# A three-part sequence kernel on one core: the matrix inversion on diagonal blocks of 64, the attention mask written in the scores' tiles, and a new order of the work

## The chip, the cores and the metric

The kernel runs on one core of a Trainium2 chip. Its engines work side by side, each through its own list of instructions in order: TensorE (PE: matrix products and transposes, with PEld for its weight loads), VectorE (DVE), ScalarE (ACT), GpSimd (POOL), and SyncE (SP), which here only issues transfers. They wait for one another by semaphores. Products land in PSUM, which has eight banks; everything else is in SBUF. The metric is the device time of one execution in microseconds (us). Lower is better.

## The reference, cut to what matters

Input is `x` of 2048 tokens by 128 features, all float32. Two parts follow each other:

```python
x = x + layernorm(scan(layernorm(x), W0, Wkv, bkv, eta))
x = x + layernorm(net(layernorm(x), ...))
# scan over the 2048 tokens, one after the other:
y = xt @ W.T;  err = y - vt;  W = W - eta * 2/128 * (err.T @ xt)
# net: 6 layers, 16 heads of 64, window 32
for i in range(6):
    x = attn(shift(x)) + x        # q, k: l2norm, scale, rotary; scores in windows of 32
    x = ffn(shift(x)) + x         # layernorm, W1, a * gelu(gate), W2
# in the attention:
sim = where(mask, -max, q @ k.T * 8);  out = softmax(sim) @ v;  out = out @ Wo
```

The scan updates a 128x128 matrix by one token at a time. The kernel does it in 16 chunks of 128 tokens: inside a chunk the token by token dependence is a unit lower triangular system, and its 128x128 matrix has to be inverted once for each chunk.

## The kernel before, in words

A chunk or tile is 128 tokens; there are 16 tiles, in four groups of four.

**Start.** Tokens are normalised and transposed, and `gram` forms each chunk's matrix of inner products. The triangular matrices of the 16 chunks are inverted together by doubling: six rounds (`ROUNDS`), each with `below(r, g)` (a product with the masked part `c_b`, made by GpSimd), a copy of the product by ScalarE (`c_q`), `update(r, g)` (two products, for the inverse and its transpose, `c_mm`), and a subtraction on VectorE. `targets` makes the values of the scan on the way. In the last round only one of the two is updated. `apply_x` and `apply_v` use the inverses, and the short chain `chain_w`, VectorE `chain_u`, `chain_d`, VectorE `chain_W` walks through the 16 chunks, four before the main loop and four each in its first three steps (`chunk_at`).

**Main loop.** 96 tile visits (6 layers of 16 tiles) and 14 more steps to run out. Each engine's body is one list written by hand; `t = s - lag` says which tile a piece serves, so one pass through the list works on several tiles at once. For each tile TensorE does: `project` (k halves, then q halves, four products 128x128 by 512 columns into `psq`), `turn` twice (the normalised k and q are transposed, T0 to T3), `values` for the four windows (U0 to U3), `mask` and `scores` into `pss`, `turn_p` (P0, P1), and `mix` (Y). For each group of four tiles it does once: transposes F and X, six `hidden` products (gates G0 to G2, and A0 to A2), and `narrow` (Z). `merge` makes a layer's 16 combined value and output matrices from `mvT` and `wo` as four banks H0 to H3, once a layer.

The mask is a product that starts the accumulation in each half of `pss`: in `mask`, two bf16 products of 512 columns, with 32 rows and 128 output partitions each (a tile's shape of 32x128 on the array), or with the identity for the first tile of a layer. The 64 products of `scores` then accumulate onto it, in the shape 64x32: two halves of the rows by four quarters of the columns, eight positions. Products with the same shape but different positions can run at once on the array; `values` and `mix` use 128x32, the turns and merges 64x128, `project`, `hidden` and `narrow` the whole 128x128.

**Buffers.** Outside `psq` and `pss` (two banks each) four banks form a ring. `take` gives them out in TensorE's order, so the bank of a product is that of four products before, and TensorE waits until ScalarE or VectorE has emptied it (`freed`). `psq` is held by the k halves until VectorE has read it twice (lines 782 and 785) and ScalarE has squared it (1167), then by the q halves (841, 857, 1062).

**The roots.** The norms' inverse roots for 32 heads of q and k: ScalarE makes a first guess from the bits of the sum (line 1094, `SEED`), and GpSimd refines it by ten small operations, lines 1269 to 1287, each waiting for the one before. Then GpSimd scales k and q (1290, 1294).

**ScalarE's tables.** Exp (1134) and Gelu (1158) need different function tables, and the compiler puts a table load before a use whose table is not in place. The three Gelus of a group stand together, behind the Exp of their step.

## Time and profile before

| | |
|---|---|
| median of 3 runs | 1675.6 us (1674.8 to 1677.26) |
| the profiled execution: its time, its span | 1674.12 us, 1672.3 us |
| mean granted TensorE clock | 0.985 of full speed |
| PE, busy and share of the span | 1591.6 us, 95% |
| DVE | 1253.5 us, 75% |
| ACT | 1080.7 us, 65% |
| POOL | 1386.3 us, 83% |
| PEld (weight loads, beside PE) | 938.3 us, 56% |

A row of a timeline gives the start in the span, the duration of the piece, the engine, the line, what is written from what, the shape on the array (rows*columns) and the count of instructions in the piece. A float32 product or weight load is two instructions here. Consecutive pieces overlap a little, since a product's end is modelled; what a piece costs is the difference between its start and the next one's. The bracket at the end is the idle time before the piece and who ended it.

### The profile page before, as it was taken

Reading aid. Unit: us, or ns where it says so; the run is one execution under the profiler, and the core shown is the slowest. Engines: PE = TensorE matmul, PEld = TensorE weight load, DVE = VectorE, ACT = ScalarE, POOL = GpSimd, SP = SyncE. Lnnn points to the kernel's source line nnn. Section 1 sums busy time; section 2 is a strip of 40 time slices with the busy share of each in tenths; the row PEclk is TensorE's granted clock in tenths of the full one; section 3 lists DMA queues with packets and bytes.
Section 4 is the critical chain, followed back from the end, with each engine's and each line's share of the span. In section 5 each row is a group of like instructions: output and inputs, shape, how many; then the busy total and the mean of one; then the engine's idle time right before and its main releaser. Section 6 shows DMA issues by size and latency. Waiting matters only on the chain.

```text
span 1672.3 us, 67208 instructions
## 1 busy us (share of the span) xinstructions
PE 1591.6 (95%) x29072; PEld 938.3 (56%) x29072; DVE 1253.5 (75%) x1683; ACT 1080.7 (65%) x1843; POOL 1386.3 (83%) x1726
## 2 busy tenths in 40 slices
PE   5986899999999999999999999999999999999994
PEld 4963455655555555565555555555555555555552
DVE  5447777777787787787787787777777787778863
ACT  3234766767766776766766767676766766766661
POOL 6318898988988988988998988988998998988971
PEclk9987999999999999999999999999999999999998
DMA  5000000010000010000010000010000000000000
GB/s 191 2 26 1 28 9 8 3 59 9 3 22 9 3 59 9 3 21 9 3 59 9 3 22 9 3 59 9 3 22 9 2 10 9 4 21 9 7 11 26
DMA packets 24534, 32.70 MB, mean 20 GB/s; under 512 B 2372, under 2 KB 21424, under 8 KB 23344
## 3 DMA queue, kind: packets, MB, share of 16 engines
q1 hardware_dynamic: 24240, 28.41, 5.2%
q8 instruction: 230, 3.77, 0.9%
q14 instruction: 64, 0.52, 0.1%
HBM read 21.06 MB, written 1.05 MB: 13 GB/s over the span
## 4 chain that ended last, share of the span: by engine, by line
PE 82%; POOL 8%; issue 5%; DVE 3%; ACT 1%; DMA 0%; SPq 0%; POOLq 0%; DVEq 0%; ACTq 0%
PE psq L245 19%; PE ring L265 18%; PE ring L253 9%; PE ring L300 9%; PE ring L310 8%; PE pss L284 7%; PE ring L317 3%; PE pss L276 1%; PE ring L326 1%; PE ring L355 1%; POOL qa L1290 1%; POOL qa L1245 1%; POOL qa L1236 1%; POOL qa L1294 1%; POOL pr L1240 1%
## 5 line engine op out<-in xcount | busy, mean ns | idle before, releaser
L245 PE MATMUL psq<-wqk,x0S 128*128 128x512 f32 x768 | 383.0, 622 | 5.5 <-ACT x0S L990 3.7
L265 PE MATMUL ring<-mh,x0S 128*32 128x512 f32 x3072 | 367.2, 595 | 0.4 <-ACT uT L1158 0.4
L1245 POOL TENSOR_TENSOR qa<-qa,qb 128x1024 f32<-128x1024 f32 x96 | 228.3, 2378 | 65.6 <-DVE qb L857 65.5
L1236 POOL TENSOR_TENSOR qa<-qa,qb 128x1024 f32<-128x1024 f32 x96 | 226.9, 2364 | 6.8 <-DVE qb L785 6.8
L245 PEld LDWEIGHTS psq<-wqk,x0S 128*128 128x128 f32 x768 | 136.1, 192 | 133.0 <-issue 117.2
L253 PEld LDWEIGHTS ring<-ident,qa 64*128 64x128 f32 x3072 | 110.5, 139 | 158.8 <-issue 104.7
L866 DVE TENSOR_REDUCE ss<-sq 128x16 f32<-128x1024 f32 x96 | 117.1, 1220 | 104.0 <-ACT sq L1062 104.0
L300 PE MATMUL ring<-u,pT 128*32 128x128 f32 x6144 | 187.6, 274 | 3.8 <-ACT pT L1129 3.5
L1290 POOL TENSOR_TENSOR qa<-qa,rn 128x1024 f32<-128x1024 f32 x96 | 182.7, 1903 | 7.5
L1240 POOL TENSOR_TENSOR pr<-pr,rden 128x1024 f32<-128x1024 f32 x96 | 184.0, 1916 | 2.0 <-DVE rden L814 2.0
L1294 POOL TENSOR_TENSOR qa<-qa,rn 128x1024 f32<-128x1024 f32 x96 | 183.2, 1908 | 0.0
L300 PEld LDWEIGHTS ring<-u,pT 128*32 128x32 f32 x6144 | 162.0, 110 | 27.2 <-issue 27.2
L284 PEld LDWEIGHTS pss<-kT,qT 64*32 64x32 f32 x12288 | 127.9, 105 | 83.3 <-issue 82.2
L782 DVE TENSOR_TENSOR qa<-psq,tab 128x1024 f32<-128x1024 f32 x96 | 117.2, 1221 | 75.4 <-PE psq L245 75.2
L1051 ACT COPY qT<-ring 128x512 f32<-128x512 f32 x96 | 56.3, 586 | 157.3 <-PE ring L253 157.3
L265 PEld LDWEIGHTS ring<-mh,x0S 128*32 128x32 f32 x3072 | 87.9, 109 | 123.1 <-issue 107.4
L841 DVE TENSOR_TENSOR qa<-psq,tab 128x1024 f32<-128x1024 f32 x96 | 117.2, 1221 | 51.1 <-PE psq L245 51.1
L310 PE MATMUL ring<-xh,w 128*128 128x512 f32 (+1 forms) x288 | 146.7, 620 | 1.4 <-ACT xh L1147 0.9
L284 PE MATMUL pss<-kT,qT 64*32 64x64 f32 x12288 | 144.5, 226 | 3.3 <-issue 3.3
L253 PE MATMUL ring<-ident,qa 64*128 64x64 f32 x3072 | 136.7, 229 | 6.4 <-POOL qa L1290 5.3
L1062 ACT ACTIVATE sq<-psq 128x1024 f32<-128x1024 f32 x96 | 98.3, 1023 | 67.7 <-DVE qb L857 67.7
L1167 ACT ACTIVATE sq<-psq 128x1024 f32<-128x1024 f32 x96 | 97.8, 1018 | 65.6 <-DVE qb L785 65.6
(161 smaller groups left out, 3005.1 us busy)
## 6 DMA issues: line engine op xcount, KB each, us to landing
wqk<-in_wqk SPq DMA_DIRECT2D x6, 1024.0 KB, 4.8
mvT<-in_mvT SPq DMA_DIRECT2D x6, 512.0 KB, 3.6
wo<-in_wo SPq DMA_DIRECT2D x6, 512.0 KB, 5.0
xf<-x SPq DMA_DIRECT2D x24, 128.0 KB
xf<-x SPq DMA_DIRECT2D x24, 127.0 KB
rope<-in_rope SPq DMA_DIRECT2D x1, 2048.0 KB, 10.2
w<-in_w SPq DMA_DIRECT2D x6, 341.0 KB, 7.1
xmid<-in_x SPq DMA_DIRECT2D x4, 256.0 KB, 5.4
```

The lines of the kernel that those rows point to most:

```text
L245: return mm(psq[:, 512 * (n % 2):512 * (n % 2) + 512], x0S[:, tile * P:tile * P + P], wqk[:, l % 2, 512 * n:512 * n + 512], start=True, st ...
L253: last = tr(banks[r][:, 64 * blk:64 * blk + 64], src(blk)[rows], ident[rows, rows])
L265: last = mm(bank[WIN * g:WIN * g + WIN, :], x0S[:, tile * P + WIN * w:tile * P + WIN * w + WIN], mh[:, l % 2, g, :, :].rearrange("p j n -> ...
L284: last = mm(pss[WIN * w:WIN * w + WIN, 512 * r + KEYS * pair:512 * r + KEYS * pair + KEYS], qT[rows, pair, WIN * w:WIN * w + WIN], kT[rows ...
L300: last = mm(bank[WIN * w:WIN * w + WIN, 0:P], pT[:, half, b * P + WIN * w:b * P + WIN * w + WIN], u4[:, slot, v_w, b * P:b * P + P], start ...
L310: return mm(bank[0:n, :], w1[:, col:col + n], xnT[:, :], start=True, stop=True)
L782: v.tensor_tensor(a3[t % 2][:, 16:32, :], q3, tab[:, t % 2, 2, :].unsqueeze(1).broadcast_to([P, HEADS, HD]), ALU.mult)
L1236: g_.tensor_tensor(qa[:, t % 2, 1024:2048], qa[:, t % 2, 1024:2048], qb[:, 1024:2048], ALU.add).then_inc(sum_k, 1)
L1240: g_.tensor_tensor(p4[t % 2], p4[t % 2], rden[:, :].unsqueeze(1).unsqueeze(3).broadcast_to([P, 2, HEADS, WIN]), ALU.mult).then_inc(p_ready, 1)
L1245: g_.tensor_tensor(qa[:, t % 2, 0:1024], qa[:, t % 2, 0:1024], qb[:, 0:1024], ALU.add).then_inc(sum_q, 1)
L1290: g_.tensor_tensor(a3[t % 2][:, 16:32, :], a3[t % 2][:, 16:32, :], rn[:, 16:32].unsqueeze(2).broadcast_to([P, HEADS, HD]), ALU.mult).then_ ...
L1294: g_.tensor_tensor(a3[t % 2][:, 0:16, :], a3[t % 2][:, 0:16, :], rn[:, 0:16].unsqueeze(2).broadcast_to([P, HEADS, HD]), ALU.mult).then_inc ...
```

## The change

Nine pieces, made together:

1. **Inversion.** The doubling rounds 0 to 4 work on the two 64x64 diagonal blocks of each chunk's matrix alone. `c_mm`, `c_q`, `c_b` and the level masks are half as wide. The two blocks sit in rows 0 to 63 and 64 to 127 and write the same PSUM bank at their own partitions. The last round makes the lower left block from the two finished inverses (one product with rows 64 to 127 into partitions 0 to 63, one more, and a negation), written into `c_inv`, which GpSimd clears before.
2. **Mask.** `mask` is eight products in the scores' shape 64x32 instead of two in 32x128, each with the same 512 columns. It stands directly ahead of `scores`, without the identity product.
3. **Merges.** They come in pairs, (H0, H1) and (H2, H3), with the row halves alternating product by product.
4. **Roots.** The guess's refinement is a product of two quadratics: ScalarE does the guess, a square (1201), two more squares with a bias (1214, 1215) and two scaled copies (1218, 1220); GpSimd does three products (1308, 1318, 1320).
5. **Order.** All lists of the main loop are put in another order with other lags; the loop has 17 more steps to run out instead of 14, of which the first four serve nothing on TensorE.
6. **Gelus.** The three Gelus of a group are spread over one step, with the Exp between the first and the second.
7. **Constants.** `s_const` is split in three; ScalarE and VectorE wait for the identity, `eta` and the levels apart. The levels' transfer is half as large. TensorE still begins with a wait for `s_const`, which now covers three transfers, the last of them still `bv`.
8. **Mask rows.** The first tile's mask differs only in window 0.
9. **End.** The final layer norm's small tiles have a place for each group, so that groups do not wait for each other.

`project` keeps whole 128x128 squares.

```diff
@@ constants
-SEED = float(0x5F1FFFF9)
-R_C0, R_C1 = 2.38924456, 0.703952253
-R_STEPS = 10
+SEED = float(0x5F3759DF)
+RA, RB, RC, RD, R4 = 0.4517456106905988, 1.5027395617164994, 2.121015328620893, 0.7667312148036857, 0.2740586127947685
+BLK = P // 2
@@ mask
-                for h in range(2):
-                    if t % TILES == 0:
-                        mm(pss[:, 512 * h:512 * h + 512], ident16[:, :], mask16[:, 1, :], start=True, stop=False)
-                    else:
-                        rows = slice(WIN * h, WIN * h + WIN)
-                        mm(pss[:, 512 * h:512 * h + 512], rep16[rows, :], mask16[rows, 0, :], start=True, stop=False)
+                for w in range(NWIN):
+                    for r in range(2):
+                        rows = slice(HD * r, HD * r + HD)
+                        mm(pss[WIN * w:WIN * w + WIN, 512 * r:512 * r + 512], rep16[rows, WIN * w:WIN * w + WIN],
+                           mask16[rows, int(t % TILES == 0 and w == 0), :], start=True, stop=False)
@@ merge
-                rows = slice(HD * (j % 2), HD * (j % 2) + HD)
                 for k in range(4):
-                    pair = 4 * (j // 2) + k
-                    last = mm(bank[:, k * P:k * P + P], mvT[rows, pair, :], wo[rows, pair, :], start=True, stop=True)
+                    for j, (bank, n) in zip(what, banks):
+                        rows = slice(HD * (j % 2), HD * (j % 2) + HD)
+                        pair = 4 * (j // 2) + k
+                        last = mm(ring[bank][:, k * P:k * P + P], mvT[rows, pair, :], wo[rows, pair, :], start=True, stop=True)
@@ below
-                    last = mm(rbank[g][:, k, :], c_b[r % 2][:, g, k, :], c_mm[:, g, 1, k, :], start=True, stop=True)
+                    if r < ROUNDS - 1:
+                        for rows in BOTH:
+                            last = mm(rblock[g][rows, k, :], c_b[r % 2][rows, g, k, :], c_mm[rows, g, 1, k, :], start=True, stop=True)
+                    else:
+                        last = mm(rblock[g][LO, k, :], c_g[HI, g, 1, k, :], c_inv[HI, g, k, HI], start=True, stop=True)
@@ update
+                        for rows in BOTH:
+                            mm(blocks[g][rows, 0, k, :], c_q[rows, g, k, :], c_mm[rows, g, 0, k, :], start=True, stop=True)
+                        for rows in BOTH:
+                            last = mm(blocks[g][rows, 1, k, :], c_mm[rows, g, 0, k, :], c_q[rows, g, k, :], start=True, stop=True)
+                    else:
+                        last = mm(blocks[g][LO, 1, k, :], c_mm[LO, g, 0, k, :], c_q[LO, g, k, :], start=True, stop=True)
@@ roots on GpSimd (ten operations before)
+                    g_.tensor_tensor(rb[:, :], ra[:, :], ssc[:, :], ALU.mult).then_inc(rb_ready, 1)
...
+                    g_.tensor_tensor(rp[:, :], rf1[:, :], rf2[:, :], ALU.mult).then_inc(rp_ready, 1)
+                    g_.tensor_tensor(rn[:, :], rg[:, :], rp[:, :], ALU.mult).then_inc(rn_ready, 1)
@@ roots on ScalarE
+                    nc.scalar.activation(ra[:, :], rg[:, :], ACT.Square).then_inc(rg_ready, 1)
...
+                    nc.scalar.activation(rs1[:, :], rb[:, :], ACT.Square, bias=rcon[:, 0:1]).then_inc(rs_ready, 1)
+                    nc.scalar.activation(rs2[:, :], rb[:, :], ACT.Square, bias=rcon[:, 1:2]).then_inc(rs_ready, 1)
+                    nc.scalar.activation(rf1[:, :], rs1[:, :], ACT.Copy, bias=RB)
+                    nc.scalar.activation(rf2[:, :], rs2[:, :], ACT.Copy, bias=R4 * RD, scale=R4).then_inc(rf_ready, 1)
```

TensorE in the middle of a layer, before: `psq<-wqk,x0S` is a pair of `project` products, `ring<-ident,qa` a turn of k or q, `ring<-ident,pr` the turn of the probabilities, `ring<-mh,x0S` values, `ring<-u,pT` the mix, `ring<-xh,w` the hidden products.

```order
L265 MATMUL ring<-mh,x0S 32x512 x12
L284 MATMUL pss<-kT,qT 32x64 x64
L310 MATMUL ring<-xh,w 128x512
L253 MATMUL ring<-ident,pr 128x64 x16
L245 MATMUL psq<-wqk,x0S 128x512 x2
L276 MATMUL pss<-mask,rep 128x512 x2
L300 MATMUL ring<-u,pT 32x128 x32
L265 MATMUL ring<-mh,x0S 32x512 x4
L253 MATMUL ring<-ident,qa 128x64 x16
```

The same stretch after the change:

```order
L274 MATMUL ring<-mh,x0S 32x512 x12
L283 MATMUL pss<-mask,rep 32x512 x8
L292 MATMUL pss<-kT,qT 32x64 x64
L262 MATMUL ring<-ident,pr 128x64 x16
L254 MATMUL psq<-wqk,x0S 128x512 x2
L318 MATMUL ring<-xh,w 85x512
L274 MATMUL ring<-mh,x0S 32x512 x4
L308 MATMUL ring<-u,pT 32x128 x32
L325 MATMUL ring<-w,uT 128x128 x12
L262 MATMUL ring<-ident,qa 128x64 x16
```

The mask has moved from between a projection and the mix to directly ahead of the scores, and the hidden products stand beside projections.

ScalarE in the step with the Gelus (`uT<-ring,par`), before: `pr<-pr` is the Exp, `sq<-psq` a square of the norms.

```order
L1110 COPY pT<-ring 128x8x64
L1129 COPY pT<-ring 128x8x64
L1134 ACTIVATE pr<-pr 128x1024
L1158 ACT_TABLE_LOAD
L1158 ACTIVATE uT<-ring,par 128x512 x2
L1158 ACTIVATE uT<-ring,par 85x512
L1167 ACTIVATE sq<-psq 128x1024
```

After:

```order
L1228 COPY pT<-ring 128x8x64
L1071 ACT_TABLE_LOAD
L1071 ACTIVATE uT<-ring,par 128x512
L1088 COPY u<-ring 128x512
L1096 ACTIVATE sq<-psq 128x1024
L1100 ACT_TABLE_LOAD
L1100 ACTIVATE pr<-pr 128x1024
L1107 COPY kT<-ring 128x8x64
L1113 COPY kT<-ring 128x8x64
L1126 ACT_TABLE_LOAD
L1126 ACTIVATE uT<-ring,par 128x512
```

The Exp now stands between two Gelus, so that the tables change four times a group instead of twice (the fourth load comes with the next step's Exp).

TensorE at the last round of the inversion and the start of the chain, before: `ring<-qa,u` is `below`, `psq<-qb,qa` and `pss<-qb,qa` are `update`, the rest `apply_x`, `apply_v` and the chain.

```order
L355 MATMUL ring<-qa,u 128x128 x16
L372 MATMUL psq<-qb,qa 128x128 x4
L372 MATMUL pss<-qb,qa 128x128 x4
L388 MATMUL ring<-qa,wqk 128x128 x4
L396 MATMUL ring<-x0T,qa 128x128 x4
L409 MATMUL ring<-wT,xh 128x128
```

After:

```order
L376 MATMUL ring<-qa,sq 64x64 x16
L391 MATMUL psq<-qb,qa 64x64 x8
L407 MATMUL ring<-qa,wqk 128x128 x4
L415 MATMUL ring<-x0T,qa 128x128 x4
L391 MATMUL pss<-qb,qa 64x64 x8
L428 MATMUL ring<-wT,xh 128x128
```

The sequence is the same, with products of 64 columns and one quarter of the array.

## Rows read from the trace of the kernel before

**Rows 1.** Windows, fifth layer: us, busy PE, PEld, DVE, ACT, POOL (count), clock, DMA share, GB/s.

```profile
1134.87:1382.42 247.55, 246.76 (x4721) 140.47 (x4720) 194.31 (x240) 173.03 (x293) 220.25 (x273) 1.00 0.03 9
```

**Rows 2.** Timeline of PE in the third layer: start, duration, line, out<-in, shape, count.

```profile
812.82 1.98 PE L245 MATMUL psq<-wqk,x0S 128*128 128x512 f32 x4
814.74 0.72 PE L253 MATMUL ring<-ident,qa 64*128 64x64 f32 x16
815.38 2.78 PE L265 MATMUL ring<-mh,x0S 128*32 128x512 f32 x24
818.10 1.48 PE L284 MATMUL pss<-kT,qT 64*32 64x64 f32 x128
819.51 0.71 PE L253 MATMUL ring<-ident,pr 64*128 64x64 f32 x16
820.15 2.84 PE L310 MATMUL ring<-xh,w 128*128 128x512 f32 x6
822.83 1.88 PE L245 MATMUL psq<-wqk,x0S 128*128 128x512 f32 x4
824.64 0.39 PE L276 MATMUL pss<-mask,rep 32*128 32x512 bf16 x2
824.96 1.96 PE L300 MATMUL ring<-u,pT 128*32 128x128 f32 x64
826.73 1.04 PE L265 MATMUL ring<-mh,x0S 128*32 128x512 f32 x8
827.70 0.71 PE L253 MATMUL ring<-ident,qa 64*128 64x64 f32 x16
828.34 1.98 PE L245 MATMUL psq<-wqk,x0S 128*128 128x512 f32 x4
830.16 1.02 PE L310 MATMUL ring<-xh,w 128*128 128x512 f32 x2
```

**Rows 3.** Timeline of PE, from a merge to the next projection.

```profile
913.67 0.93 PE L326 MATMUL ring<-wo,mvT 64*128 64x128 f32 x6
...
915.24 1.12 PE L245 MATMUL psq<-wqk,x0S 128*128 128x512 f32 x2
```

**Rows 4.** Timeline of ACT, the step with the Gelus.

```profile
819.85 0.23 ACT L1094 ACTIVATE rn<-ssc 128x32 int32<-128x32 int32 x1
820.25 0.58 ACT L1110 COPY pT<-ring 128x512 f32<-128x512 f32 x1 [0.18 <-PE ring L253]
820.73 0.59 ACT L1129 COPY pT<-ring 128x512 f32<-128x512 f32 x1
822.24 1.06 ACT L1134 ACTIVATE pr<-pr 128x1024 f32<-128x1024 f32 x1 [0.91 <-DVE pr L899]
823.31 1.28 ACT L1158 ACT_TABLE_LOAD   x1
824.61 1.83 ACT L1158 ACTIVATE uT<-ring,par 128x512 f32<-128x512 f32 x3
827.13 1.02 ACT L1167 ACTIVATE sq<-psq 128x1024 f32<-128x1024 f32 x1 [0.69 <-DVE qb L785]
```

**Rows 5.** Timeline of DVE, the second reading of `psq` for k.

```profile
825.89 1.21 DVE L785 TENSOR_TENSOR qb<-psq,tab 128x1024 f32<-128x1024 f32 x1
```

**Rows 6.** Timeline of ACT at the start: its second group of tokens.

```profile
15.60 1.65 ACT L953 ACTIVATE wqk<-xmid,anmr,arstd 128x128 f32<-128x128 f32 x4 [6.94 <-POOL anmr L1201]
```

**Rows 7.** Timeline of PE at the start: the inversion.

```profile
34.85 1.58 PE L355 MATMUL ring<-qa,u 128*128 128x128 f32 x8 [3.44 <-DVE qa L692]
...
45.69 3.74 PE L355 MATMUL ring<-qa,u 128*128 128x128 f32 x32
...
88.57 3.74 PE L355 MATMUL ring<-qa,u 128*128 128x128 f32 x32
...
113.59 3.78 PE L245 MATMUL psq<-wqk,x0S 128*128 128x512 f32 x4 [0.84 <-ACT x0S L990]
```

**Rows 8.** Timeline of DVE, the first of four sets before the rounds.

```profile
20.95 1.41 DVE L687 SCALAR_TENSOR_TENSOR qa<-psq,coef,mh 128x512 f32<-128x512 f32 x2 [5.04 <-ACT sq L966]
```

More of the change, by code:

```diff
@@ L427, in features @@
                 last.then_inc(filled[bank], 1)
[L429 to L434 removed]
+            pe.wait_ge(s_ident, 16)
             turn_in(0)
@@ L576, in _ @@
                     project(t, 1).then_inc(pq_done, 1)
[L577 to L584 removed]
+                t = s - 5
                 if 0 <= t < STEPS:
```

944 lines of the change are left out of this document (488 added, 456 removed).

## The prediction

> **What bounds the kernel now.** I read the windows of a middle layer first: PE is busy 246.76 of 247.55 us, POOL 220, DVE 194, ACT 173 [rows 1]. So for six layers the products themselves set the time, PE waits under 1 us a layer, and an edit is worth what it takes off PE's list, as long as no other engine makes PE wait anew. Next the timeline of PE [rows 2], read as differences of starts: a projection pair costs 1.92 between two turns and 1.81 or 1.82 where one neighbour has its own shape; a change of the array's shape costs about 0.10. Turns cost 0.64, U1 to U3 2.72, the scores 1.41, three hidden pairs 2.68, the mask 0.32, the mix 1.77, U0 0.97. Last the start [rows 7, 8]: the first projection begins at 113.59; from 45.69 to 88.57 PE works through four rounds of the inversion, 42.88 or 10.72 a round, and before, until 34.85, it waits for DVE, whose operations on 512 columns begin at 20.95. What follows the last row of the main loop is latency of one chain, which the change hardly touches.
>
> The profiled execution took 1674.1 with a span of 1672.3; the sum goes by 1674.1, and the median shown is 1.5 higher. A difference under 0.2% is no change here.
>
> **The steady part.**
>
> *Mask.* Before, the step has nine changes of shape; now eight, because the mask shares the scores' shape and U1 to U3, cut across two steps, stay together. The mask's own streams are 512 columns either way: 0.32 now, of which 0.10 is the change of shape and 0.22 the two products side by side. Eight products in eight positions: the scores run 128 instructions of 64 columns in 1.41, 11 ns each, which only overlap in all eight positions allows. So I take 0.22 for the mask and gain 0.10, for 96 tiles -9.6. The bounds: 0 gained, if eight starts at 11 ns show; a loss up to 8 times 0.22 less 0.32, 1.44 a tile, if they run one by one. I take the end near the scores' row.
>
> *Group pieces.* A1 leaves its place between scores and turn (one change of shape less), Z goes between mix and turn (one more), the other hidden products stand beside projections or each other: 0. A merge costs 1.57 less a turn of 0.64, so 0.93 [rows 3, 2]. Its four products use one half of the rows. Alternated with its partner's, the pair should take about one merge, since the turns run both halves together (16 instructions in 0.64): 0.90, and 0.10 for the new change of shape. 1.86 becomes 1.00, ten times in the loop: -8.6. Bounds +1.0 (no overlap) and -9.6.
>
> *Order of waits.* What PE can wait for now: `psq` needs 0.11, two readings by DVE of 1.21 (the second starts 1.14 after the first) and 1.02 on ACT after a projection, about 3.5 [rows 4, 5]; between k and q halves PE has U0, mix and turn, 0.86 + 1.87 + 0.64, and a hidden pair, transposes or Z in each step, so at least 4.3; after the q halves over 5.4. Covered. The roots leave POOL: ten small operations become three; at the 0.23 of ACT's operation of that size [rows 4] and 0.1 for each hand-over, seven less are about 2.3 of POOL's 13.8 a step (220.25 by 16) [rows 1], and its wait on ACT lies before the next turn with over 1 us to spare. Without that cover a turn would start later by what is missing.
>
> *ACT in the Gelu step* is the one tight place. From the end of the probabilities' turn ACT does: 0.10, copy 0.48, four small operations 0.6 (0.23 each, partly overlapping), copy 0.61, table load 1.30, Gelu G0 0.6, copy U0 0.48; at 4.31 DVE has read `psq`; square 1.02, load 1.30, Exp 0.97, copies 0.48 and 0.61, load 1.30, Gelu G1 0.66: 10.65 [rows 4, 5]. G1's bank is the one that U1 takes, four products on in the ring. PE wants it after 1.82 + 0.96 + 0.86 + 1.87 + 0.64 + 1.8 + 1.91 + 0.64 = 10.5 (projection, G0, U0, mix, turn, G1 and A0, projection, turn). With the restart of the weight loads I take 0.3 a group, +7.2 for 24. Bounds 0, since 0.2 of ACT's sum is rounding, and +1.3 a group, should each of the 16 pieces cost 0.06 more. Behind U1, U2, U3 and the next scores queue on PE; nobody else waits for it. The second pair of loads, 2.6 a group, is otherwise in ACT's free time: about 9 to 10 us of issue a step and 14.3 in this one, under 15.5.
>
> The Trainium skill speaks against this place: "ScalarE: Activation LUTs", section "What ACT_TABLE_LOAD costs", adds a drain of about 1.38 us to each load of 1.283. The trace has the load of 1283 ns but not the drain: Exp starts at 822.24, the load at 823.31, the Gelu at 824.61 [rows 4]. By the page, two loads on this path would come 2.8 later and the sum 66 us higher; I go by the row.
>
> **The start.**
>
> *Rounds 1 to 4.* Each has 96 products before (32 `below` instructions from 45.69, then 64 for the updates), at 0.11 an instruction. Now there are twice as many, of 64 columns, in pairs on opposite corners of the array. If a pair runs together, a round is half: 5.36, -21.4 for four. Lower bound of the gain 0 (twice as many, half as long, one by one). Cover: ACT's four copies, DVE's four subtractions of 512 columns instead of 1024 (about 0.7 each) and POOL's mask products all fit in 5.4; if not, a round is longer by the missing part. I allow nothing for it.
>
> *Before the rounds.* DVE's operations begin at 20.95 and PE's wait for them ends at 34.85, 13.9 later; half as wide, half of it: -7.0. Between 34.85 and 45.69 PE does three updates of 16 instructions (5.3) that halve: -2.7. ACT's second group of tokens begins at 15.60 after 6.94 of waiting [rows 6], because DVE stood before the constants; with `s_level` ahead of the rest, and only after the second group's statistics, -3, bounds 0 and -5. *Last round:* 32 instructions of `below` (3.6 by the 0.11) and as many of `update`, each half as long: -3, a little kept back for hand-overs. GpSimd's clearing of `c_inv` lies beside round 0 and costs nothing if round 1's masks are ready 2 us later than now.
>
> Sum of the start -37.1. Bounds -16 (no overlap) and -45.
>
> *Filling of the loop.* Tiles 0 to 8 wait for the chain and for POOL; with POOL freed -2, bounds +6 and -6, since the chain's products stand elsewhere.
>
> **Sum.** 1674.1 - 9.6 - 8.6 + 7.2 - 37.1 - 2 = 1624.0. I forecast 1624.
>
> **The rivals.**
>
> *A: the diagonal blocks do not overlap.* They are different rows of the array and write one PSUM bank, which no pair in the trace does: scores and turns put their two row halves into two banks [rows 2]. Then rounds cost 10.7 as before, +21.4, and with the updates of round 0, +2.7: 1648. For it: no row shows such a pair. Against it: positions of the scores that share a bank (four quarters of the columns) overlap. The Trainium skill, "TensorEngine Tiling (Array Packing)", section "Gotcha 1: PSUM Pressure", says that different row tiles cannot use the same bank at once; by that rule this rival is what happens.
>
> *B: ACT is later than I add up.* 1.3 a group instead of 0.3: +24, 1648. For it: ACT's list in this step has no gap in 10 us. Against: each term is a row.
>
> *C: slower than before.* The eight mask products run one by one, or in twos. The place is between U3 and the scores, where they now stand in PE's way, and the price is 1.76 for 0.22 at the worst, +148 (1771). It decides from 51 / 96 = 0.53 a tile, that is a mask of 0.75: less than four at a time. For it: 512 columns in eight positions is a form that the trace doesn't have. Against: U1 to U3 stream 512 columns in four positions at once.
>
> *D: the change doesn't pair the merges.* Weight loads of 128 columns could follow each other: +9.6, 1634, inside the range.
>
> **How the numbers follow.** Forecast with its bounds 56% (own range 1605 to 1637); A 21%; B 12%; both A and B or other new waits of a us a step, up to no change, 5%; C 6%. Faster by over 0.2% means under 1672: all but C and the outer part of the mixed case, 93%; within 0.2% 2%; slower 5%. The range from 1602 to 1652 takes in A and B and leaves out C and the ends, under 2 in 10.
>
> **What would show it.** Right: first projection at about 76; rounds 5.4 apart on PE; from mask to scores 0.22; from a merge pair to the values 1.0; windows of a layer 244 to 245 with PE busy but for a wait at U1 named as ACT, about 0.3, four times a layer; the span's end the same distance from the last projection. A shows as rounds of 10 us, B as longer waits at U1 behind ACT's Gelu, C as a mask of over 0.75. Wrong would be waits on POOL or on `psq` in every step: then the order costs more than the shapes give.

## The result, and the profile after

The changed kernel takes 1620.78 us (median of four runs, 1619.38 to 1621.38); the kernel before, run beside it, 1676.43. The ratio is 0.9666, with a 95% interval of 0.9649 to 0.9682: 3.3% faster. The forecast was 1624.0 with a range of 1602 to 1652. The profiled executions took 1619.38 and 1674.12, with spans of 1617.6 and 1672.3, so there are 54.7 us to account for.

The number was right, the account behind it only in part: that the sum came within 4 us is in part luck, as the stages below show. First the start. The columns are start, duration, engine, line, operation, tiles, count and, in brackets, the idle time before and what ended it.

```profile
10.55 2.23 PE L348 MATMUL ring<-ident,wqk 128*128 128x128 f32 x8 [10.55 <-DMA mh<-in_bv]
...
31.00 2.08 PE L374 MATMUL ring<-qa,u 64*64 64x64 f32 x64
...
36.65 2.03 PE L374 MATMUL ring<-qa,u 64*64 64x64 f32 x64
...
42.40 2.08 PE L374 MATMUL ring<-qa,u 64*64 64x64 f32 x64
...
53.46 0.27 PE L376 MATMUL ring<-qa,sq 64*64 64x64 f32 x1
...
75.58 0.66 PE L445 MATMUL ring<-ident,x0T 128*128 128x128 f32 x2 [4.43 <-ACT x0T L1009]
...
78.98 3.62 PE L254 MATMUL psq<-wqk,x0S 128*128 128x512 f32 x4
```

The first projection comes at 78.98 instead of 113.59 [rows 7], 34.6 earlier. Rounds begin 5.65 and 5.75 apart instead of 10.72, and the last one at 53.46. What answers to [rows 8] and [rows 6] are these rows, of VectorE and of ScalarE, whose first two groups of tokens now follow each other without a gap:

```profile
15.51 0.88 DVE L704 SCALAR_TENSOR_TENSOR qa<-psq,coef,mh 128x256 f32<-128x256 f32 x2 [4.75 <-ACT sq L995]
```

```profile
8.43 3.18 ACT L982 ACTIVATE wqk<-xmid,anmr,arstd 128x128 f32<-128x128 f32 x8
```

Then a middle layer, from the mask of its first tile to that of the next layer's, the stretch that answers to [rows 1]. The columns are the stretch, its length, each engine's busy time with its instructions, the granted clock of TensorE, the DMA share and GB/s.

```profile
1095.73:1341.77 246.04, 243.32 (x4820) 139.84 (x4816) 194.45 (x241) 199.91 (x381) 195.72 (x161) 1.00 0.03 9
```

TensorE is busy for 3.4 us less than in [rows 1], but the layer is only 1.5 shorter: its idle time went from 0.8 to 2.7. And this is the best layer of four. Where it waits is in the list of waits of the whole execution (who waited, for whom, us in total, times, the longest).

```profile
PE ring L274 <- ACT uT L1126: 7.4, 23, 0.4
...
PE pss L292 <- issue: 4.6, 7, 1.7
...
PE ring L262 <- issue: 4.4, 6, 1.5
...
PE psq L254 <- issue: 3.1, 3, 1.5
```

The first row is the wait at U1's bank that the forecast counted (7.2). The other three have no releaser: TensorE stood still with nothing on the chip's other engines to wait for, 12 us in 16 places. These are called pauses from here on. The kernel before has such rows too, about 5.4 in all (the largest reads 3.3 us at the scores, in six pauses of at most 0.9). One pause of the changed kernel, in the timeline of TensorE that answers to [rows 2]:

```profile
815.01 2.78 PE L274 MATMUL ring<-mh,x0S 128*32 128x512 f32 x24
817.72 0.41 PE L283 MATMUL pss<-mask,rep 64*32 64x512 bf16 x8
817.95 1.39 PE L292 MATMUL pss<-kT,qT 64*32 64x64 f32 x120
821.05 0.32 PE L292 MATMUL pss<-kT,qT 64*32 64x64 f32 x8 [1.71 <-issue]
821.30 0.71 PE L262 MATMUL ring<-ident,pr 64*128 64x64 f32 x16
821.94 1.98 PE L254 MATMUL psq<-wqk,x0S 128*128 128x512 f32 x4
```

The mask takes 0.23 to the scores, as forecast; the scores then stop 8 instructions, which are four products, before their end.

To compare kernels I cut each profiled execution at four starts on TensorE: the first projection, and the mix (L308, before L300) of tiles 0, 20 and 84. The stretch from tile 20 to tile 84 is four layers. Its "undisturbed" length is worked out: the steps repeat every eight tiles, each of the eight kinds is taken at its second shortest length, times eight. What is over is pauses.

| us | to first projection | to mix 0 | to mix 20 | four layers (undisturbed) | to the end |
|---|---|---|---|---|---|
| before | 113.6 | 60.1 | 312.6 | 990.2 (984.9) | 195.9 |
| after | 79.0 | 55.5 | 300.8 | 987.9 (977.3) | 194.3 |
| e1 inversion alone | 76.4 | 59.5 | 311.6 | 985.0 (984.8) | 197.0 |
| e2 mask in two products | 78.9 | 53.6 | 299.1 | 986.8 (984.8) | 194.1 |
| e3 merges in turn | 81.0 | 55.7 | 301.7 | 991.1 (981.8) | 193.9 |
| e7 roots on GpSimd | 78.7 | 53.8 | 310.8 | 992.1 (977.4) | 198.5 |
| e8 64 transposes ahead | 86.6 | 57.8 | 300.1 | 990.6 (977.2) | 194.4 |
| e9 the same on e2 | 85.5 | 55.7 | 299.4 | 990.3 (984.7) | 195.6 |
| e11 32 transposes | 81.4 | 55.6 | 300.8 | 988.0 (977.4) | 194.7 |

So of the 54.7 us, 34.6 are won before the first projection, 4.5 up to the first mix, 11.8 in the filling of the loop, only 2.2 in four steady layers, and 1.6 in the rest (from the starts before they were rounded).

Each row of the table is one execution, and executions of one kernel differ by 1.5 to 8 us (the largest spread is that of e5 below, 1618.67 to 1626.83). A difference of one or two us between two rows of a column is therefore not shown by them. The undisturbed lengths repeat much better: 977.2 to 977.4 in the four kernels with the changed loop and its shapes, 984.7 and 984.8 in the two with the mask in two products.

### The profile page after: what moved, and what is told of

Same layout as the page of the kernel before. It is cut to its first block, busy times and chain, and to the rows that moved or that the text cites. A ratio compares the mean times of both kernels' runs of the same rounds, so it can differ in the third digit from the quotient of the medians.

```text
span 1617.6 us, 69676 instructions
## 1 busy us (share of the span) xinstructions
PE 1544.3 (95%) x30224; PEld 907.8 (56%) x30224; DVE 1234.8 (76%) x1693; ACT 1232.5 (76%) x2368; POOL 1222.1 (76%) x1051
## 3 DMA queue, kind: packets, MB, share of 16 engines
q8 instruction: 239, 3.92, 1.0%
## 4 chain that ended last, share of the span: by engine, by line
PE 75%; ACT 7%; issue 5%; DVE 3%; POOL 1%; DMA 0%; ACTq 0%; SPq 0%; POOLq 0%; DVEq 0%
PE ring L274 20%; PE psq L254 18%; PE ring L262 9%; PE ring L308 8%; PE pss L292 7%; PE ring L325 4%; PE ring L318 4%; PE pss L283 2%; DVE qb L927 2%; ACT L1126 2%; ACT sq L1096 1%; ACT uT L1126 1%; ACT pr L1100 1%; ACT kT L1107 1%; PE ring L649 1%
## 5 line engine op out<-in xcount | busy, mean ns | idle before, releaser
L308 PEld LDWEIGHTS ring<-u,pT 128*32 128x32 f32 x6144 | 172.9, 111 | 61.4 <-issue 61.4
L308 PE MATMUL ring<-u,pT 128*32 128x128 f32 x6144 | 187.0, 274 | 3.2 <-ACT pT L1228 3.2
L274 PEld LDWEIGHTS ring<-mh,x0S 128*32 128x32 f32 x3072 | 80.0, 109 | 190.5 <-issue 172.6
L821 DVE TENSOR_REDUCE den<-pr 128x16 f32<-128x1024 f32 x96 | 116.5, 1214 | 62.8 <-ACT pr L1100 62.8
L292 PEld LDWEIGHTS pss<-kT,qT 64*32 64x32 f32 x12288 | 139.3, 105 | 10.9 <-issue 5.8
L887 DVE TENSOR_REDUCE mx<-pss 128x16 f32<-128x1024 f32 x96 | 117.2, 1221 | 16.1 <-PE pss L292 15.8
L1096 ACT ACTIVATE sq<-psq 128x1024 f32<-128x1024 f32 x96 | 98.4, 1025 | 34.8 <-DVE qb L927 34.6
L865 DVE TENSOR_REDUCE ss<-sq 128x16 f32<-128x1024 f32 x96 | 117.1, 1220 | 3.8 <-ACT sq L1172 1.2
```

Source lines behind the costliest of these rows:

```text
L274: last = mm(bank[WIN * g:WIN * g + WIN, :], x0S[:, tile * P + WIN * w:tile * P + WIN * w + WIN], mh[:, l % 2, g, :, :].rearrange("p j n -> ...
L292: last = mm(pss[WIN * w:WIN * w + WIN, 512 * r + KEYS * pair:512 * r + KEYS * pair + KEYS], qT[rows, pair, WIN * w:WIN * w + WIN], kT[rows ...
L308: last = mm(bank[WIN * w:WIN * w + WIN, 0:P], pT[:, half, b * P + WIN * w:b * P + WIN * w + WIN], u4[:, slot, v_w, b * P:b * P + P], start ...
```

## The experiments

Each starts from the changed kernel unless it says otherwise. Ratios are to the kernel before on the same chip, with 95% intervals.

**e1: the inversion alone.** The kernel before, with the diff's pieces on `gram`, `below`, `update`, `c_inv`, the level tables, the constants and their loads, and no others. To the kernel before, for example:

```
-                for k in range(QUAD):
-                    last = mm(rbank[g][:, k, :], c_b[r % 2][:, g, k, :], c_mm[:, g, 1, k, :], start=True, stop=True)
+                for k in range(QUAD):
+                    if r < ROUNDS - 1:
+                        for rows in BOTH:
+                            last = mm(rblock[g][rows, k, :], c_b[r % 2][rows, g, k, :], c_mm[rows, g, 1, k, :], ...)
```

> The kernel before with nothing of the change but the inversion on diagonal blocks of 64 (with the earlier constants that go with it). Theory: the start is worth what the two traces show, 113.59 to 78.98 at the first projection (34.6 us), less a few us, since the first merges stay unpaired (about 1.5): the first projection at 79 to 82, layer 0 from its first projection to that of layer 1 still 260, and 1676.4 - 33 = 1643 in all (1640 to 1646). Rival 1: layer 0's shorter time in the changed kernel (247.0 instead of 260.1) comes from the start too (an engine clock or buffers that are ready earlier): then 1643 - 13 = 1630. Rival 2: the start gains only together with the paired merges and the shared roots: above 1650.

Measured: 1631.15, ratio 0.9727 (0.9708 to 0.9745). The first projection stands at 76.42:

```profile
76.42 3.44 PE L252 MATMUL psq<-wqk,x0S 128*128 128x512 f32 x4 [0.84 <-ACT x0S L1012]
```

That is 37.2 earlier than before; the forecast's sum for the start was 37.1. Filling stays long (311.6), which refutes rival 1, although the total is near the one that it names. The total is 12 us under what I expected. In the profiled execution some 4 of that is the start, and 5.2 are in the four layers: the loop is the old one, product for product, but its pauses are gone (985.0 of 984.8 undisturbed). The windows view of a stretch of it about a layer long:

```profile
1143.90:1390.30 246.40, 246.07 (x4714) 139.41 (x4713) 194.55 (x241) 172.88 (x292) 220.51 (x273) 1.00 0.03 9
```

So an identical loop ran 1.3 us a layer faster behind a different start. All the rest of the change (mask, merges, roots, order) is then worth 1631.15 - 1620.78, 10 us.

**e2: the mask in two products.**

```
-                for w in range(NWIN):
-                    for r in range(2):
-                        rows = slice(HD * r, HD * r + HD)
-                        mm(pss[WIN * w:WIN * w + WIN, 512 * r:512 * r + 512], rep16[rows, ...], mask16[rows, ...], ...)
+                for h in range(2):
+                    ...
+                        rows = slice(WIN * h, WIN * h + WIN)
+                        mm(pss[:, 512 * h:512 * h + 512], rep16[rows, :], mask16[rows, 0, :], start=True, stop=False)
```

> The changed kernel with the mask in two products on 32 rows as before, at the new place (U3, mask, scores). Theory of the forecast: the only price is a further change of the array's shape, so from mask to scores 0.32 instead of 0.23, +0.10 for 96 tiles: +9.6, 1620.8 + 9.6 = 1630.4 (1628 to 1632). Rival: the eight products with their 8 weight loads cost by themselves what the change of shape saves (a layer gained only 0.5 us, not 1.8): then 1621 or less, and the trace shows 0.23 to 0.25 from mask to scores here too.

Measured: 1616.26, ratio 0.9639 (0.9621 to 0.9657). Not slower, and rather faster. The theory's time missed; the rival's time came, but without the row that it asked for (0.23 to 0.25). The rows:

```profile
812.99 0.39 PE L286 MATMUL pss<-mask,rep 32*128 32x512 bf16 x2
813.31 1.48 PE L294 MATMUL pss<-kT,qT 64*32 64x64 f32 x128
```

From mask to scores it is 0.32, and the undisturbed four layers are 7.5 longer for 64 tiles: 0.12 a tile, where the forecast's term was 0.10. But the real four layers are not longer than with eight products (1.1 shorter), because pauses fall from 10.6 to 2.0. What the shape of the eight products gives, pauses take back at this position of the program.

**e3: the merges in turn.**

```
-                for k in range(4):
-                    for j, (bank, n) in zip(what, banks):
+                for j, (bank, n) in zip(what, banks):
+                    for k in range(4):
```

> The changed kernel with the two merges of a pair one after the other at the same place, four products each, instead of alternating. Theory: alternating is what makes the halves of the array's rows work side by side; the pair goes from 1.09 to 0.93 + 0.93 = 1.86 or a little less, ten pairs in the loop and two at the start: +8 to +9, 1629 (1627 to 1631). Rival: the queue of products is deep enough to overlap the two groups of four anyway, or the pair was bound by its weight loads: 1621 to 1623, and the pair at 1.1.

Measured: 1625.91, ratio 0.9693 (0.9674 to 0.9712), +5.1, between the theory (1627 to 1631) and the rival (1621 to 1623). The two intervals overlap, so the rows decide. First two rows of the changed kernel, which answer to [rows 3], then two of this one:

```profile
636.60 1.16 PE L338 MATMUL ring<-wo,mvT 64*128 64x128 f32 x16
637.70 1.06 PE L274 MATMUL ring<-mh,x0S 128*32 128x512 f32 x8
```

```profile
639.35 1.71 PE L338 MATMUL ring<-wo,mvT 64*128 64x128 f32 x16
640.99 1.07 PE L274 MATMUL ring<-mh,x0S 128*32 128x512 f32 x8
```

1.10 alternating, 1.64 in turn: 0.54 a pair, and 4.5 in the undisturbed four layers, which have eight pairs. Alternating does overlap the halves of the rows, but not wholly (1.10 for a pair against 1.00 forecast). In turn the pair costs 1.64 and not the 1.86 of two merges before; why was not tried.

**e4: the diagonal blocks in turn.**

```
-                for k in range(QUAD):
-                    if r < ROUNDS - 1:
-                        for rows in BOTH:
-                            last = mm(rblock[g][rows, k, :], ...)
+                if r < ROUNDS - 1:
+                    for rows in BOTH:
+                        for k in range(QUAD):
+                            last = mm(rblock[g][rows, k, :], ...)
```

and the same in `update`.

> The changed kernel with the products of a round ordered by block: first all four of the upper 64 rows, then all of the lower, instead of alternating between the two corners of the array. The same products on the same banks. Theory: the alternation is what lets a pair run together on one PSUM bank (0.029 an instruction, rounds 5.6 to 5.75 apart); in turn they run one by one at about 0.055, so the four rounds take some 43 instead of 22.5 and round 0's updates 2.7 more: +20 to +24, 1643 (1638 to 1647). Rival: a shorter product (64 rows and columns) is simply half as long whatever stands beside it: then nothing changes, 1621 (to 1624).

Measured: 1633.80, ratio 0.9739 (0.9723 to 0.9755), +13.0. First projection at 92.05, 13.1 later. Rows at the beginning of rounds 2, 3 and 4:

```profile
42.47 0.22 PE L374 MATMUL ring<-qa,u 64*64 64x64 f32 x1
...
50.70 0.27 PE L374 MATMUL ring<-qa,u 64*64 64x64 f32 x1
...
59.03 0.27 PE L374 MATMUL ring<-qa,u 64*64 64x64 f32 x1
```

They are 8.2 and 8.3 apart, against 5.7 alternating. The order of the same products on the same banks is worth 2.6 a round: products in opposite corners of the array run side by side although they write one bank. The size says so too: a round of 192 instructions in 5.7 us is 0.030 for one, and half of what an instruction of twice the columns took before would be 0.055. In turn they take less than the 10.7 that I had for "one by one"; why a block's own products still overlap in part was not tried.

**e5: two operations less on ScalarE.** `rf1` and `rf2` computed on GpSimd.

```
-                    nc.scalar.activation(rf1[:, :], rs1[:, :], ACT.Copy, bias=RB)
-                    nc.scalar.activation(rf2[:, :], rs2[:, :], ACT.Copy, bias=R4 * RD, scale=R4).then_inc(rf_ready, 1)
+                    g_.tensor_scalar(rf1[:, :], rs1[:, :], RB, None, ALU.add)
+                    g_.tensor_scalar(rf2[:, :], rs2[:, :], R4, R4 * RD, ALU.mult, ALU.add).then_inc(rf_ready, 1)
```

> The changed kernel with the two affine pieces of the roots (rf1, rf2) on GpSimd instead of ScalarE; nothing else. Theory: ScalarE's unbroken list in the Gelu step is 0.25 shorter (0.13 and 0.14 between starts), so the wait of TensorE for U1's bank falls from 0.32 to 0.05 a group: -6.5, 1614 (1612 to 1616), with that wait gone from the list of waits and no other in its place. Rival 1: the wait is made by something else that ends at the same time (the probabilities' turn, the square): it stays at 7.4 in all and the time at 1621. Rival 2: GpSimd's two operations more (0.25 each) make the turns wait: above 1621.

Measured: 1621.37, ratio 0.9673 (0.9647 to 0.9699), no change, and the wait at U1 still 7.4 in all. The timeline of its ScalarE in a Gelu step, laid out as [rows 4], shows why. First two rows of the changed kernel, the first Gelu and the copy of U0, then the step in e5:

```profile
714.14 0.69 ACT L1071 ACTIVATE uT<-ring,par 128x512 f32<-128x512 f32 x1
714.88 0.59 ACT L1088 COPY u<-ring 128x512 f32<-128x512 f32 x1
```

```profile
905.95 0.69 ACT L1071 ACTIVATE uT<-ring,par 128x512 f32<-128x512 f32 x1
906.97 0.59 ACT L1088 COPY u<-ring 128x512 f32<-128x512 f32 x1 [0.34 <-PE ring L274]
907.48 1.02 ACT L1096 ACTIVATE sq<-psq 128x1024 f32<-128x1024 f32 x1
908.52 1.28 ACT L1100 ACT_TABLE_LOAD   x1
909.82 1.06 ACT L1100 ACTIVATE pr<-pr 128x1024 f32<-128x1024 f32 x1
...
913.15 0.69 ACT L1126 ACTIVATE uT<-ring,par 128x512 f32<-128x512 f32 x1
```

What was taken off is given back as 0.34 of waiting for U0: the copy starts 1.02 behind the Gelu's start, and 0.74 in the changed kernel. From that copy to the start of the second Gelu it is 6.18 here and 6.17 there. The list that binds begins at U0, not at the probabilities' turn. My 10.65 against 10.5 had nearly the right difference from the wrong beginning.

**e6: the load moved.** The load of the next layer's `wqk`:

```
-                if s % TILES == 0 and 1 <= l < LAYERS - 1:
+                if s % TILES == 6 and 1 <= l < LAYERS - 1:
```

> The changed kernel with the load of the next layer's query and key weights (1 MB) six steps later in SyncE's list; it is needed only a layer on. Three of TensorE's pauses of 1.5 to 1.7 us (at 325.98, 572.92 and 821.05) stand right behind that transfer. Theory 1: the transfer holds up the reads of TensorE's instructions; moved, the three pauses go: -4.7, 1616. Theory 2: the pauses come from where the 16 KB reads of instructions fall in TensorE's program; then the transfer's place changes nothing, and pauses stand at the same instructions: 1621 (1620 to 1622). For theory 2: e3 and e4, whose loops have as many instructions, have them at the same places, while e1 and e2, with other counts, have hardly any.

Measured: 1622.97, ratio 0.9672 (0.9650 to 0.9695), no change. The pauses moved. Rows of e6:

```profile
819.82 0.32 PE L292 MATMUL pss<-kT,qT 64*32 64x64 f32 x8 [0.69 <-issue]
...
865.78 0.31 PE L292 MATMUL pss<-kT,qT 64*32 64x64 f32 x6 [1.71 <-issue]
```

The changed kernel has 1.71 at the first of these places (821.05) and 0.61 at the second (865.92). The changed kernel issued the load at 814.47, shortly before the first, e6 at 858.66, shortly before the second; there are new ones of 1.06 and 1.60 at 617.50 and 1115.23 too, each 7 us behind the moved load's issue. Of the three pauses that the expectation names, those at 572.92 and 821.05 fell from 1.52 to 0.20 and from 1.71 to 0.69, but the one at 325.98 kept 1.32 of its 1.49 without the load. So each theory had half: the places come from the program, and a 1 MB transfer beside one made it 1.0 to 1.6 us longer at five places, and hardly at a sixth.

**e7: all of the roots on GpSimd**, in the ten operations of before, where its first piece now stands; only the seed on ScalarE.

```
-                    g_.tensor_tensor(rb[:, :], ra[:, :], ssc[:, :], ALU.mult).then_inc(rb_ready, 1)
+                    g_.tensor_tensor(ra[:, :], rg[:, :], rg[:, :], ALU.mult).then_inc(r_step, 1)
+                    pool.wait_ge(r_step, n + 1)
+                    g_.tensor_tensor(rb[:, :], ra[:, :], ssc[:, :], ALU.mult).then_inc(r_step, 1)
+                    ...
```

> The changed kernel with the roots as before the change, ten small operations in a row on GpSimd and only the seed on ScalarE, at the place where GpSimd now has its first piece. It tells whether layer 0's shorter time (247.0, where the kernel before and e1 have 260.1 and 258.5) comes from the shared roots or from the new order. Theory 1 (roots): layer 0 is near 258, the steady layers unchanged but for the U1 wait that goes since ScalarE is freed (-7): 1625. Theory 2 (order): layer 0 stays at 247 to 249 and the U1 wait goes: 1614 to 1616. Rival: GpSimd (76% busy, then 90%) makes a turn wait in each group: above 1630.

Measured: 1635.28, ratio 0.9753 (0.9733 to 0.9773), +14.5, the rival's time, though the turns wait in the filling more than in each group. Filling is 310.8, as in the kernel before and e1. The two rows of its list of waits on GpSimd's normalization, and, from its page, the busy times (GpSimd 1374 where the changed kernel has 1222):

```profile
PE ring L263 <- POOL qa L1325: 12.4, 14, 4.1
...
PE ring L263 <- POOL qa L1351: 2.3, 2, 1.1
```

```profile
PE 1551.7 (95%) x30224; PEld 909.5 (56%) x30224; DVE 1236.1 (76%) x1693; ACT 1149.1 (70%) x1888; POOL 1373.9 (84%) x1723
```

Sharing the roots, which I had costed at nothing with -2 for filling, is worth 10 in the filling, 4 in the four layers and 4 behind them in the profiled execution, less 2 before the first mix. Most of the filling's part is this one wait, at the keys' turn, 7.8 of its 12.4 before the mix of tile 20. The 4 in the four layers are not a price of each step, for the undisturbed length is the same (977.4); 2.3 of them are this wait. Windows of tiles 4 to 7, the kernel before, e7 and the changed kernel, show that GpSimd (the fifth busy time) is all but full there:

```profile
187.94:249.02 61.08, 55.13 (x1142) 29.98 (x1140) 46.24 (x65) 41.55 (x77) 57.29 (x73) 0.97 0.02 7
```

```profile
149.80:210.19 60.39, 53.53 (x1177) 30.33 (x1174) 47.76 (x59) 40.90 (x73) 55.66 (x71) 1.00 0.02 7
```

```profile
146.61:202.72 56.11, 53.42 (x1176) 30.35 (x1173) 47.25 (x59) 43.65 (x94) 49.48 (x43) 1.00 0.03 8
```

94% busy before, 92% in e7 and 88% in the changed kernel, and PE 90%, 89% and 95%. The granted clock is 0.97 in the first window, but 1.00 in e7, which is nearly as long: the clock does not explain it.

Two of the pieces are thus worth 14.5 and 5.1 (e3) inside the new order, but all that e1 lacks is worth 10. By that difference, an estimate, the other pieces together cost some 9 us; the wait at U1 alone is 7.4. The new order without the other pieces, and the shared roots in the old order, were not run.

**e8, e9, e11: the program shifted.** 64 or 32 transposes of 64 x 64, of no use, ahead of TensorE's first; e9 is on e2.

```
+            for k in range(64):
+                tr(ring[3][0:64, 0:64], ident[0:64, 0:64], ident[0:64, 0:64])
             turn_in(0)
```

> The changed kernel with 64 small transposes (64 x 64, on a bank that is not used yet) before TensorE's first one, in time in which it waits anyway; they do no work. Theory: they shift the whole program against the borders of the 16 KB instruction reads by half a read, so the pauses without a releaser (17, 12.4 us in all in the changed kernel) stand elsewhere and sum to something else, 2 to 12: 1611 to 1621, most likely 1615; the steps between pauses stay as they are. Rival: the pauses belong to the work (banks, transfers, weights): the same 12 us at the same products, 1621.

> e2 (the mask in two products, 1616.3, with hardly a pause) with the same 64 small transposes ahead of TensorE's first product as e8. Theory: e2's lack of pauses is the place of its 16 KB instruction reads and not a property of two products; shifted by half a read (128 instructions, two to a product) the borders fall into the dense stretch of mask, scores and turn as often as in the changed kernel. From the distances of those borders in e2's trace: pauses +6 to +9, so 1616.3 + 8 = 1624 (1621 to 1627), and four layers (mix of tile 20 to mix of tile 84) 993 to 996 instead of 986.8. Rival: two products leave the stretch too short for a pause wherever the borders are: 1616 to 1618.

> The changed kernel as in e8, with 32 small transposes instead of 64. From the distances between every 256th instruction of TensorE in the changed kernel's trace, pauses taken out, the sum of what is missing to 2.2 us a read is 13.2 there, 15.8 for 64 products (e8, which came out 10 us slower) and 10.2 for 32. Theory: the pauses are 2 to 3 less than in the changed kernel: 1618 (1616 to 1621). Rival: any product ahead costs, whatever its number: between 1621 and 1631, about 1626.

Measured: e8 1630.92, ratio 0.9728 (0.9710 to 0.9747); e9 1627.69, 0.9701 (0.9687 to 0.9716); e11 1620.72, 0.9656 (0.9640 to 0.9672). They cannot be read by their totals, for my premise was wrong: the transposes did not run in waiting time.

```profile
10.32 1.91 PE L450 MATMUL ring<-ident 64*64 64x64 f32 x16 [10.32 <-DMA mh<-in_bv]
...
17.28 1.97 PE L348 MATMUL ring<-ident,wqk 128*128 128x128 f32 x8
```

TensorE's list opens with a wait for the constants (until 10.3), so the 64 put the start off by 6.7 (17.28 against 10.55), and 32 by 3.4. The four layers are free of that. Against its own base e8 has 2.7 more and e9 3.5 more, at undisturbed lengths that did not change (977.2 for 977.3, 984.7 for 984.8); e9 stays short of the 993 that I forecast, and e11's are 988.0 (977.4), no less than its base, so its -3 does not show there: the distances of the borders, and the 2.2 us that its expectation measures them by, give the sign of a large shift, not its size. Pauses thus depend on the position of the program, in size and place. e9 has 5.6 of them where e2 has 2.0: the two products' calm was in part luck.

**e10: A0 behind the turn**, on e2. VectorE's use of A0 moves behind its two readings of the query projection as well.

```
                     hidden(ring[bank], 1, 1).then_inc(filled[bank], 1)
-                    bank, n = take("A0", i)
-                    wait(pe, freed[bank], n)
-                    hidden(ring[bank], 0, 0).then_inc(filled[bank], 1)
...
                     turn([ring[bank] for bank, n in banks], t, 0)
+                i = group_at(s, 13)
+                if i >= 0:
+                    bank, n = take("A0", i)
+                    wait(pe, freed[bank], n)
+                    hidden(ring[bank], 0, 0).then_inc(filled[bank], 1)
```

> e2 with the hidden product A0 not in front of the query projection but behind the turn of the queries, between it and U1, and VectorE's use of it behind its two readings of that projection. No instruction is added. Theory: TensorE has 0.96 of other work before it wants U1's bank, so the wait of 0.32 in each group goes; one more change of shape costs 0.10: -0.2 for 24 groups, -5, 1611 (1609 to 1614), with no wait for the Gelu in the list. Rival 1: VectorE's use of A0, now later, delays the square sums and with them the next key projection: above 1618. Rival 2: a new wait at the turn of the queries (its banks come one earlier in the ring): 1616 or more.

Measured: 1618.64, ratio 0.9646 (0.9632 to 0.9661). Nothing is won, although the wait is all but gone from the list (0.3, once). Rows of TensorE, then the Gelu that U1's bank waits for:

```profile
715.56 0.71 PE L263 MATMUL ring<-ident,qa 64*128 64x64 f32 x16
...
719.62 1.12 PE L320 MATMUL ring<-xh,w 128*128 128x512 f32 x2
720.87 2.78 PE L275 MATMUL ring<-mh,x0S 128*32 128x512 f32 x24
```

```profile
720.12 0.69 ACT L1131 ACTIVATE uT<-ring,par 128x512 f32<-128x512 f32 x1
```

The Gelu ends at 720.81 and U1 starts at 720.87, so U1 still waits for it. What is left of the wait, 0.12, is too short to be listed. From the turn behind the mix to U1 it is 5.31 here (715.56 to 720.87) and 5.31 in e2 (711.52 to 716.83): as in e5, ScalarE's list from U0 on sets the time, and where TensorE does its other work does not matter. The undisturbed layers are 985.0 for 984.8.

**e12: e2 without TensorE's first wait**, the version that should be fastest, with more rounds: `wait(pe, s_const, 16 * NCONST)` at the head of TensorE's list is left out, since `targets` has it.

```
             mm, tr = nc.tensor.matmul, nc.tensor.transpose
-            wait(pe, s_const, 16 * NCONST)
```

> e2 with TensorE's first wait, for the last of the constants (the rows of e2, e8 and e11 show it until 10.3 to 10.6), taken out; the first product then waits for the identity and ScalarE's first four tokens, and the constants are waited for where they are first used. The version that should be the fastest, run again with more rounds. Theory: ScalarE's first group is done at about 10.15, so 0.4 less at the start; the place of the instruction reads moves by nothing that matters, so the loop is e2's: 1615.9 (1613 to 1618), first product at 10.2. Rival: e2's 1616.3 was within the scatter of the changed kernel's 1620.8 (their intervals touch): then 1619 to 1621.

Measured: 1618.54, ratio 0.9651 (0.9637 to 0.9666), between theory and rival. TensorE now starts at 10.2, behind ScalarE, as meant. The loop is e2's (987.1, 985.0 undisturbed). e2, e10 and e12 all lie under the changed kernel's 0.9666, by 0.0015 to 0.0027, but each interval touches the changed kernel's. The mask in two products is at least as good; that it is faster is likely and not shown.

## Why the prediction was right, point by point

- *The start, -37.1:* right. e1 shows -37.2, the changed kernel -34.6; its own order puts more of layer 0's chain ahead of the first projection and gives it back before the first mix (55.5 for 60.1). Within the term things were exchanged: from 45.69 to 88.57 it was 42.9 and is 22.5 (31.00 to 53.46), 20.4 for the forecast 21.4; the part up to round 1 gained 14.7, not 12.7 (-7.0, -2.7 and -3); the last round, from its first product to the chain's first, gained 2.1 of the forecast 3 (88.57 to 97.65 before, 53.46 to 60.48 now). From there to the first projection the changed kernel needs 2.6 more (18.5 for 15.9). The chain's first product, before and now:

```profile
97.65 0.39 PE L409 MATMUL ring<-wT,xh 128*128 128x128 f32 x2
```

```profile
60.48 0.49 PE L428 MATMUL ring<-wT,xh 128*128 128x128 f32 x2
```

- *Mask, -9.6:* the size is right (0.12 a tile undisturbed, e2), the effect on the time is not: against e2, none of it shows in the result. One such product of 512 columns on the whole array takes 0.23 to the next start (e2, the first tile of a layer), and eight in eight positions take 0.23 too: all eight run at once. The scores' row did not show that: at 11 ns an instruction, where one of 128 columns took 0.116 in the merges, five to six at once would do.
- *Merges, -8.6:* 1.10 a pair for 1.86, so -7.6 for ten. e3 shows that 0.54 a pair is from alternating.
- *ScalarE in the Gelu step, +7.2:* 7.4 measured. Right in size, wrong in the path (e5), and no cheaper way round it was found (e10). Half of the 0.3 a group was allowed for the weight loads' restart; no run shows that price, for U1 starts 0.06 behind the Gelu's end (e10).
- *Roots and `psq` cover, 0; filling, -2:* the step that failed. The cover was counted in the middle layers. In the filling GpSimd's list is nearly as long as the step, and a delay of it reaches a turn: from the first projection to the mix of tile 20 TensorE waited 3.9 us for GpSimd's `qa` before, waits 8.9 in e7, with the roots back on GpSimd, and 0.2 in the changed kernel. Sharing the roots is worth 14.5 in the new order (e7), where the forecast had 0 for it and 2 for the filling. How much of the 11.8 it would give in the old order is open: the waits named there come to 3.9.
- *What no term held:* pauses without a releaser. In four layers they went from 5.3 (990.2 less 984.9) to 10.6, which took 5.3 of the 7.6 that the shapes gave there. The trace of before could have warned me: its waits named issue come to about 5.4.
- *The sum:* the start gave 2.5 less than forecast. The forecast for mask, merges and ScalarE is 8.5 for the 64 tiles of the four layers, and they gave 2.2. The filling and the stretch before the first mix gave 16.3 where 2 was forecast. That these made up for one another is luck.
- *Rivals:* A is refuted by e4 and by rounds 5.7 apart. The rule of the Trainium skill, "TensorEngine Tiling (Array Packing)", section "Gotcha 1: PSUM Pressure", that different row tiles cannot use the same bank at once, does not hold for these: the corners write different partitions of one bank, and run together. B and D did not happen. C decides from a mask of 0.75; the mask was 0.23.
- The table load's drain, of "ScalarE: Activation LUTs", section "What ACT_TABLE_LOAD costs" in the Trainium skill, does not appear in the step of e5 either: Exp starts at 909.82, behind a load of 1.28 from 908.52 on.

**The pauses.** The page counts the packets of the queue that brings instructions. First the kernel before, then the changed one:

```profile
q8 instruction: 230, 3.77, 0.9%
```

```profile
q8 instruction: 239, 3.92, 1.0%
```

3.92 MB in 239 packets is 16.4 KB each. The trace of the changed kernel holds 61233 of TensorE's instructions (products, weight loads and its sequencer's), 239.2 times 256, and that of the kernel before 58950, 230.3 times 256. In all fourteen kernels the whole part of this quotient is the number of packets. So a packet brings 256 instructions, of 64 bytes each. Number TensorE's instructions in the order of their starts: the 16 pauses of the changed kernel from the first mix on stand at numbers 193 to 195 modulo 256, every one. So do the 18 of e8, the 13 of e11, the 6 of e9, the 3 of e2, and 11 of the 12 of the kernel before. Only e12 differs: of its seven, the two longest (1.14 and 0.35) stand at 192 and 190, and five of 0.16 elsewhere. The pauses are thus at the borders of the packets. In 15 of those 16 the 256 instructions before the pause were used up in 1.6 to 2.0 us (in one, in 3.0), where the mean of the loop is 6.5. The scores issue 256 instructions in 1.41 us, 16 of the mask before and 32 of the turn behind.

Shown: the place at a border, the change with position (e1, e8, e9), the part of the 1 MB load at most places (e6). That the reading of instructions is what stops TensorE is inferred from the place, and no run changes the reading itself. That eight products make more pauses than two, because the dense stretch is 12 instructions longer, fits (10.6, 13.4 and 10.6 at three positions against 2.0 and 5.6 at two), but five positions don't show it.

## What to carry to other kernels

Where TensorE is the bound and its products are short, count instructions as well as us: a stretch that uses up 256 instructions in about 2 us can run out of them, and then a finer cut with the better shape gains nothing. An engine at 90% of a steady step (GpSimd, 220 of 248 us) can be the bound in the filling, whatever cover the steady step has; look at each stage before an edit that relieves it is costed at nothing. And when a loop's time moves by a few tenths of a per cent after an edit outside it, compare undisturbed steps before looking for a cause in the loop.

## What the runs showed of the hardware

- Products on opposite corners of the array, 64 rows and 64 columns each, overlap although they write one PSUM bank: rounds of 5.7 us alternating, 8.3 in turn (e4).
- The alternation matters for halves of the rows too: a pair of merges takes 1.10 us alternating and 1.64 in turn (e3).
- A change of the array's shape costs 0.12 us (e2, undisturbed layers).
- At the borders of the 16 KB packets of instructions TensorE can stand still for 0.2 to 2.1 us (the longest in e8), and beside a 1 MB load for 1.0 to 1.6 us more at five of six places (e6).
- TensorE's granted clock is 1.00 in the first 20 us, where it is busy for 8.94, but 0.75 on average (between its levels of 1.2 and 2.4 GHz) from 80 to 100 in the changed kernel, where it is busy for 13.95 in single products of the chain. It is back at 1.00 in the window of tiles 4 to 7 above, from 146.61 on. The two stretches:

```profile
0.00:20.00 20.00, 8.94 (x154) 7.56 (x156) 9.45 (x52) 11.64 (x25) 10.76 (x24) 1.00 0.81 287
80.00:100.00 20.00, 13.95 (x34) 7.00 (x32) 14.12 (x33) 6.11 (x15) 10.64 (x15) 0.75 0.00 0
```
